# The bias of the base product, times the gate, added to the residual stream by GpSimd instead of being multiplied in on TensorE

## The reference

```
x = x + ga * attention(...)            # output projection o @ wo, then the gate
h = layernorm(x) * (1 + cb) + sb
base = h @ base_W.T + base_b           # base_b: one row of 512
probs = softmax(h @ router_W.T + router_b)      # 15 columns, the best 8 are kept
w = sum over the kept columns of each of the 8 experts
lora = ((h @ A) * w) @ B * 2           # 8 experts of rank 16: 128 columns
x = x + gb * (base + lora)             # gb: one row of 512 for each element
```

## Time and profile before

| what | us |
|---|---|
| median of 3 runs | 1971.87 (1970.68 to 1974.28) |
| the profiled execution's own time | 1970.33 |
| its span, from first to last instruction | 1968.6 |
| TensorE busy in the span | 1896.1 |
| VectorE busy | 1515.9 |
| GpSimd busy | 907.3 |
| ScalarE busy | 928.3 |

### The profile page before, as it was taken

One profiled execution on the slowest core, in us unless ns is written; L12 is line 12 of the kernel. 1 busy time (PEld: TensorE's weight loads), 2 busy tenths in 40 slices (PEclk: granted clock), 3 DMA queues, 4 the chain that ended last, 5 costly groups with the idle time before them and its releaser, 6 DMA issues.

```text
span 1968.6 us, 41786 instructions
## 1 busy us (share of the span) xinstructions
PE 1896.1 (96%) x14040; PEld 1621.9 (82%) x14040; DVE 1515.9 (77%) x2386; ACT 928.3 (47%) x2297; POOL 907.3 (46%) x872
## 2 busy tenths in 40 slices
PE   8999979999999999999999999998999989998998
PEld 3688869999999999999999999987898856666786
DVE  2577757777877877878878877888889558889886
ACT  1233334444444444444444444455545368888332
POOL 0133354444444444444444444363576557887111
PEclk9999989999999999999999999999999989999999
DMA  9577751111111111111111111322387765553121
GB/s 345 167 233 247 232 160 48 48 48 48 43 44 41 48 48 48 48 48 48 43 41 44 48 48 46 113 67 60 116 251 221 230 215 162 157 158 111 41 62 59
DMA packets 201695, 211.02 MB, mean 107 GB/s; under 512 B 19066, under 2 KB 172666, under 8 KB 200604
## 3 DMA queue, kind: packets, MB, share of 16 engines
q1 hardware_dynamic: 200692, 209.27, 34.4%
q10 hardware_dynamic: 936, 0.85, 0.1%
HBM read 128.14 MB, written 73.53 MB: 102 GB/s over the span
## 4 chain that ended last, share of the span: by engine, by line
PE 75%; issue 11%; DVE 8%; POOL 3%; SPq 1%; DMA 1%; ACT 1%; POOLq 0%; DVEq 0%; ACTq 0%
PE ps L1037 18%; PE ps L998 18%; PE ps L1012 7%; PE ps L1026 4%; PE ps L1049 4%; DVE f_neg_max L1991 4%; PE ps L1811 3%; PE ps L1021 3%; PE ps L2604 2%; POOL k_rot L571 2%; PE ps L2568 2%; PE ps L2106 2%; PE ps L1819 2%; PE ps L2162 2%; PE ps L2112 1%
## 5 line engine op out<-in xcount | busy, mean ns | idle before, releaser
L1037 PE MATMUL ps<-wo,ot 128*128 (+1 forms) x1536 | 387.2, 401 | 0.1
L1037 PEld LDWEIGHTS ps<-wo,ot 128*128 128x128 f32 x1536 | 281.0, 189 | 60.1 <-issue 1.3
L998 PE MATMUL ps<-ht_hi,wq 128*128 (+1 forms) x2048 | 288.0, 283 | 4.9 <-DVE q_swap L870 4.9
L998 PEld LDWEIGHTS ps<-ht_hi,wq 128*128 128x128 f32 x2048 | 268.9, 192 | 10.7 <-DVE q_swap L870 5.1
L796 ACT ACTIVATE prob<-ps,neg_max 128x128 f32<-128x128 f32 (+1 forms) x512 | 208.6, 421 | 130.0 <-DVE neg_max L877 108.0
L955 POOL TENSOR_TENSOR q_rot<-q_rot,q_swap 128x512 f32<-128x512 f32 x128 | 165.1, 1290 | 197.9 <-DVE q_swap L870 193.4
L803 ACT ACTIVATE pt<-ps 128x512 fp32r<-128x512 f32 x192 | 108.1, 598 | 301.7 <-PE ps L1049 301.7
L950 POOL TENSOR_TENSOR prob<-prob,inv_sum 128x512 f32<-128x512 f32 x64 | 66.6, 1040 | 280.0 <-DVE inv_sum L886 280.0
L998 PE MATMUL ps<-ht_lo,wq 128*128 (+1 forms) x1024 | 165.4, 284 | 0.0
L1991 DVE TENSOR_REDUCE f_neg_max<-ps 128x4 f32<-128x512 f32 (+1 forms) x128 | 122.0, 957 | 41.7 <-PE ps L2106 36.8
L571 POOL TENSOR_TENSOR k_rot<-k_rot,k_swap 128x512 f32<-128x512 f32 x32 | 60.1, 1880 | 193.0 <-DVE k_swap L476 193.0
(11 more groups left out here) (248 smaller groups left out, 4150.5 us busy)
## 6 DMA issues: line engine op xcount, KB each, us to landing
stack_dram<-e_part SPq DMA_DIRECT2D x192, 128.0 KB, 2.4
v_dram<-v_part SPq DMA_DIRECT2D x32, 512.0 KB, 5.7
k_dram<-k_part SPq DMA_DIRECT2D x64, 256.0 KB, 2.5
kk<-k_dram SPq DMA_DIRECT2D x128, 128.0 KB, 2.1
vv<-v_dram SPq DMA_DIRECT2D x128, 128.0 KB, 2.1
f_q<-stack_dram SPq DMA_DIRECT2D x124, 104.0 KB
f_k<-stack_dram SPq DMA_DIRECT2D x124, 104.0 KB
wmod<-in_wmod SPq DMA_DIRECT2D x12, 1024.0 KB, 12.1
```

The lines of the kernel that those rows point to most:

```text
L998: mm = nc.tensor.matmul(ps_q[j][:, e], w[:, c:c + HD0], r[:, bass.ds(u % B, 1), k].rearrange("p o s -> p (o s)"), start=(n == 0), stop=(n ...
L1037: mm = nc.tensor.matmul(ps_y[j][:], o[:, j, h * P:(h + 1) * P], w[:, bass.ds(at + h * D, D)], start=(n == 0), stop=(n == len(passes) - 1))
```

## The change

The bias leaves TensorE. The bias row is loaded broadcast over 128 partitions. GpSimd multiplies it with the gate row gb of the element (`g_gated_bias`, 128x512) and adds the result to both tiles of the residual stream, once the norm of that element has read the stream. The products of the base group now begin with the first weight product. The gate buffer is refilled only when GpSimd has used it as well.

```
@@ tables, sync
-        sp.wait_ge(zeroed, 2)
-        sp.dma_start(bias_raw[0:1], io["base_b"]).then_inc(bias_in, 16)
-        sp.dma_start(bias_raw[32:33], io["base_b"]).then_inc(bias_in, 16)
+        sp.dma_start(bias[:], io["base_b"].partition_broadcast(P)).then_inc(bias_in, 16)
...
             sp.wait_ge(f_step, 2 * (b - 2) + 2)
+            sp.wait_ge(biased, b - 1)
             load_gb(b)
@@ scalar_side
-        if j == 9:
-            act.wait_ge(bias_in, 32)
-            nc.scalar.activation(bias[:], bias_raw[:], ACT.Identity).then_inc(hi_done, 1)
-            nc.scalar.activation(row_r[:], row[:], ACT.Identity).then_inc(hi_done, 1)
@@ vector
-        dve.wait_ge(hi_done, 11)
-        v.tensor_tensor(bias[32:33], bias_raw[32:33], f32(bias[32:33]), ALU.subtract).then_inc(lo_done, 1)
...
         dve.wait_ge(summed, B - 1)
+        dve.wait_ge(biased, B)
@@ gpsimd
-    def gpsimd_first(pool):
-        pool.wait_ge(keep.p_done, 6 * B)
-        nc.gpsimd.memset(bias_raw[:], 0.0).then_inc(zeroed, 1)
-        nc.gpsimd.memset(row[:], 1.0).then_inc(zeroed, 1)
-
     def gpsimd(pool):
-        for b in range(B - 1):
-            pool.wait_ge(f_step, 2 * b + 2)
+        pool.wait_ge(bias_in, 16)
+        for b in range(B):
             x = element(keep.acc, b)
-            nc.gpsimd.tensor_tensor(x, x, gated[:], ALU.add).then_inc(summed, 1)
+            pool.wait_ge(gb_in, 16 * max(b + 1, 2))
+            nc.gpsimd.tensor_tensor(gated_bias[:], gb[b % 2][:], bias[:], ALU.mult).then_inc(bias_step, 1)
+            pool.wait_ge(ln_step, 7 * b + 7)
+            pool.wait_ge(bias_step, b + 1)
+            nc.gpsimd.tensor_tensor(x, x, over_tiles(gated_bias[:]), ALU.add).then_inc(biased, 1)
+            if b < B - 1:
+                pool.wait_ge(biased, b + 1)
+                pool.wait_ge(f_step, 2 * b + 2)
+                nc.gpsimd.tensor_tensor(x, x, gated[:], ALU.add).then_inc(summed, 1)
@@ base
-                nc.tensor.matmul(ps_b[:, t], row_r[:], bias[:], start=True, stop=False, skip_group_check=True)
-                for a, r in split_passes(hs, w[1]):
-                    for k in range(KT):
-                        mm = nc.tensor.matmul(ps_b[:, t], a[:, k, t * P:(t + 1) * P], r[:, k], start=False, stop=False,
-                                              skip_group_check=True)
+                passes = [(a, r, k) for a, r in split_passes(hs, w[1]) for k in range(KT)]
+                for j, (a, r, k) in enumerate(passes):
+                    mm = nc.tensor.matmul(ps_b[:, t], a[:, k, t * P:(t + 1) * P], r[:, k], start=(j == 0), stop=False,
+                                          skip_group_check=True)
```

More of the change, by code:

```diff
@@ L2276, in output1 @@
     bs = [first.tile(f"g_bs{i}", [ER, D], F32R) for i in range(2)]
[L2277 to L2280, removed]
+    bias = first.tile("g_bias", [P, D])
+    gated_bias = first.tile("g_gated_bias", [P, D])
     rbias = last.tile("g_rbias", [P, NR])
@@ L2310, in output1 @@
     ga_in, gb_in = sem("g_ga_in"), sem("g_gb_in")
-    zeroed = sem("g_zeroed")
+    bias_step, biased = sem("g_bias_step"), sem("g_biased")
     hi_done, lo_done = sem("g_hi_done"), sem("g_lo_done")
@@ L2635, in tensor @@
             if b == 0:
-                pe.wait_ge(lo_done, 2 * KT + 2)
+                pe.wait_ge(lo_done, 2 * KT + 1)
                 pe.wait_ge(keep.o_split, B * KT)
@@ L2645, in output1 @@
     programs.sync, programs.scalar, programs.vector, programs.gpsimd, programs.tensor = sync, scalar, vector, gpsimd, tensor
-    programs.weights, programs.tables, programs.gpsimd_first = weights, tables, gpsimd_first
+    programs.weights, programs.tables = weights, tables
     programs.scalar_side, programs.vector_side, programs.tensor_side = scalar_side, vector_side, tensor_side
@@ L2704, in _ @@
                 first.gpsimd(pool)
-                third.gpsimd_first(pool)
                 second.gpsimd(pool)
```

## The result

The changed kernel takes 1990.28 us (median of 6 runs, 1987.06 to 1993.98), the kernel before 1971.75 us beside it (6 runs, 1970.68 to 1974.28): a ratio of 1.0092 [1.0079, 1.0105]. It is slower by 18.5 us, where 11 had been forecast (1983.0). That is inside the range of 1972 to 1997, and just above the 1977 to 1990 that the forecast gave to its own case. The profiled execution took 1989.56 us, its span is 1987.8 against 1968.6: 19.2 us more.

What follows compares the result with a forecast made beforehand. TensorE was taken as the bound (16.81 us an element), then waiting for VectorE's mid product. Start 1.0 + clock 1.7 + periods 5.6 + end 2.8 = +11.1 on 1970.3, 1981.4; median 1.5 higher, 1983.0; range 1972 to 1997.

Steps and rivals of the forecast that it cites:

- its own case: Whole kernel: GpSimd's holds make VectorE late and TensorE wait; 1983.0 us, own range 1977 to 1990, chance 0.62.
- The bias products' cost: TensorE, output stage: each bias product costs 0.61 us, two 1.22 us an element; TensorE's own period becomes 15.59 us.
- The mechanism: Output stage: GpSimd's bias addition holds VectorE's two-input subtraction g_e, 2.56 us late; TensorE waits for the mid product.
- The steps of the hold: GpSimd and VectorE, each period: multiplication ends at t = 6.99, second scaling 7.28, bias addition 9.49, g_e 9.43, mid product 14.78.
- The period at full clock: Output stage, per element: 17.92 us, 1.11 us longer than today's 16.81; over five periods 5.6 us.
- the granted clock falls inside the stage: Sign in the changed kernel's profile that would show the prediction wrong; no size given.
- the clock falls in every period: Rival: TensorE's 2.3 us waits bring 1.2 GHz, second output product 2.8 us more, five times 14 us: 1997; chance 0.10.
- The end: Element 7: no output product hides the wait, GpSimd holds its gates, the last turn starts 2.8 us later: +2.8 us.
- The start: Element 0: split of h waits for the bias addition, +1.0, plus 1.7 for half clock; -0.6 if the split goes first.
- The forecast's own case: Start of the stage: bias addition gets in ahead of VectorE's split of h, +1.0 us, and +1.7 for the clock.
- TensorE as the bound: Rival: GpSimd's operations slip past VectorE's two-input ones, delay below 0.3 us, 1962 us; chance 0.16.
- The partial hold: Rival: only one 128x512 hold of some 1.3 us reaches the mid product, period 16.7, 1973 us; chance 0.12.

Runs made afterwards that it cites:

- experiments 2 and 3: 2: changed kernel without GpSimd's bias addition, multiplication kept, 1970.32 us (0.9989); 3: changed kernel with both operations replaced by fills that read nothing, 1968.19 us (0.9979).
- experiment 5: Changed kernel with the broadcast bias load issued behind the attention, right ahead of the gate rows: 1989.61 us, 1.0091 against the kernel before.
- experiment 4: Kernel before plus only the broadcast load of the bias row to 128 partitions of an unused tile: 1973.36 us against 1971.49, 1.0012.
- experiment 7: Changed kernel run again without an edit: 1989.01 us, 1.0086 against the kernel before.

## Why the forecast held, and what it mis-sized

**What was right.** *The bias products' cost*, 0.61 us each: without them, and without GpSimd's work, the period was 15.58 (15.59 as worked out). *The mechanism*: g_e is held by the bias addition (experiments 2 and 3) and TensorE waits for what follows. *The steps of the hold*: multiplication ends at t = 7.07 (forecast 6.99), second scaling 7.35 (7.28), bias addition 9.59 (9.49), g_e 9.65 (9.43), mid product 14.99 (14.78).

**The period at full clock** was put at 17.92 and is 18.29. Two small terms: 0.21 us in the hold, and the turn, estimated at 0.30, which takes 0.44. Over five periods 1.9 us.

**The clock within the stage** is the step that failed. The forecast took TensorE's wait as free of it, and named "the granted clock falls inside the stage" as a sign of being wrong. That sign came. It had "the clock falls in every period" as a rival at 0.10 with 2.8 us each. What happened lies between: behind a wait of 2.54 us the granted clock was 0.50 in about every second period, and the slowed product then cost 1.57 us, not 2.8, since only a part of it ran at 1.2 GHz (wholly so it would take twice 2.79). Three of five make 4.7 us, and filling the wait gave 5.0 back. The two together, 1.9 + 4.7, make up the 6.5 us between 5.6 and 12.1. So the direction and the hold were worked out. That the total came as near as 7 us is in part luck: the arrival is 3.7 us above its term and the start 3.4 us below it, and the two misses cancel. That it lies within the range at all is owed to the width that the clock rival gave it.

**The end** was put at +2.8 and is +4.0. The holds of element 7's gates came as told: the chain has the comparison product and then TensorE's long wait for mid,

```profile
1972.83 2.71 DVE L1146 TENSOR_TENSOR g_cmp_b<-g_cmp_b,g_earlier 128x450 f32<-128x450 f32 x1
...
1979.21 0.69 PE L2605 MATMUL ps<-ident,g_mid 128*128 128x128 f32 x2 [4.07 <-DVE g_mid L2493]
1980.83 2.93 PE L2612 MATMUL ps<-g_bs,g_ms 128*128 128x512 f32 x6 [0.93 <-DVE g_ms L2499]
```

and before, beside the last of these rows:

```profile
1962.27 1.67 PE L2618 MATMUL ps<-g_bs,g_ms 128*128 128x512 f32 x6 [0.93 <-DVE g_ms L2506]
```

On the scale of before (1979.16 less the 15.2 us lost until element 7's output product) the mid product ends at 1964.0, where 1963.7 was worked out. The rest goes by the clock again. This last group of 6 takes 2.93 us against 1.67 (its first half, which the last operations of VectorE wait for, 1.66 against 0.99), and the turn 0.69 against 0.38, with the granted clock at 0.50:

```profile
1982.00:1983.00 1.00, 1.00 (x4) 0.81 (x3) 0.38 (x1) 0.00 (x0) 0.00 (x0) 0.50 0.00 0
```

**The start** was put at +1.0 and +1.7 for the clock, with -0.6 as the alternative if the split got in first. The alternative came (-0.7): GpSimd's first multiplication started 10.65 us behind element 0's product, where the forecast had about 10.2. The forecast's own case exists: experiment 5 shows it, at 3.7 us more than the other, close to the 2.7 + 0.6 between the two as priced.

**The arrival** was taken as unchanged, and is 3.7 us late in the profiled execution. The forecast put the new 128-partition load at nothing and gave no reason. By experiment 4 that load costs 0.6 to 4.1 us. The rest isn't shown to be the change's: the three profiles with the moved load, whose code is the same up to there, arrived between 1822 and 1829.

**The rivals.** TensorE as the bound (1962) would have needed a hold under 0.3 us; with none it was 1963.93. The partial hold (1973 at a period of 16.7) is what the multiplication alone gave: 16.56 and 1970.32. The removal was worth 1.23 us a period (16.81 to 15.58), and filling the same products from 33 to 65 or 128 rows 0.8 us.

**A reading that was wrong.** The prediction took a sentence of the Trainium skill for a price of the whole product, and held the rows against it. The Trainium skill ("TensorE: Matmul & The Clock Gate", Step-by-step: what each phase is for) says it of the time of the weight load alone, and there the trace agrees: the 33-row load takes 0.18 us, and three 128-row loads take 0.53. What is dear at 33 rows is that neither this load nor the next is hidden behind running products, the gaps of 0.37 and 0.24 us. The sum went by the rows, so the 9.8 us are untouched.

## What to carry to other kernels

Work moved from a busy engine to an idle one is only as cheap as what it holds there: look for the small two-input VectorE operations on the chain that leads back to the busy engine, and place GpSimd's reads where that engine has work of its own, as behind the mid product here. Price the consequence twice, once in waiting and once in TensorE's clock: here a wait of 2.5 us in every 18 cost another 1 us a period in the mean. And before moving a dear product away, see why it is dear: four lines of tile shapes gave as much as the best placement of the moved work.

## What the runs showed that was not expected

- The clock falls behind some of the 2.5 us waits and not behind others. In the first profile the products at 1885, 1923 and 1943 are slowed and that at 1905 isn't; in the second profile of the same kernel (experiment 7) those at 1885, 1904 and 1943 are, and that at 1924 isn't. It was three of five each time, and in experiment 5 too. What decides it is open.
- A product on 33 rows between products on 128 costs 0.42 us and 0.18 more in the 12 products behind it (2.97 against 2.79 us); on 65 rows it costs 0.23 us and nothing more (2.77 us).
- GpSimd fills, which read nothing, hold VectorE's one-input scalings of 512 columns (2.07 us the pair, 1.23 before) and not its two-input operations (0.63 us for the comparison product). So the two are not held on the same condition.
